# A state-space layer's sums over states, taken over transposed blocks instead of over identity products

## The reference, cut to what matters

```python
dA  = exp(dt[b,l,d] * A[d,n])
dBu = dt[b,l,d] * u[b,l,d] * Bm[b,l,n]
h   = dA * h + dBu                      # over the tokens l
y[b,l,d] = sum_n h[b,l,d,n] * Cm[b,l,n]
y   = y + u * Dp[d]
y   = y * silu(z)
out = einsum('bld,ed->ble', y, W_out)
return x + out
```

## Time and profile before

| | us |
|---|---|
| median of 3 runs | 2183.1 (2182.24 to 2184.62) |
| the profiled execution | 2189.44 |
| its span in the profile | 2187.7 |
| busy in the span: PE, DVE, ACT, POOL | 1903.7, 1653.2, 1273.8, 1450.1 |
| mean granted TensorE clock | 0.946 of full speed |
| the layer with the change in it | about 1060 to 1970 of the span |

### The profile page before, as it was taken

One profiled execution on the slowest core, in us unless ns is written; L12 is line 12 of the kernel. 1 busy time (PEld: TensorE's weight loads), 2 busy tenths in 40 slices (PEclk: granted clock), 3 DMA queues, 4 the chain that ended last, 5 costly groups with the idle time before them and its releaser, 6 DMA issues.

```text
span 2187.7 us, 32346 instructions
## 1 busy us (share of the span) xinstructions
PE 1903.7 (87%) x9878; PEld 1113.8 (51%) x9878; DVE 1653.2 (76%) x2282; ACT 1273.8 (58%) x2729; POOL 1450.1 (66%) x1195
## 2 busy tenths in 40 slices
PE   2599999999984699993799999999999999679998
PEld 1244444444433599992345454545453544248886
DVE  4477887887755555651399999999999999986664
ACT  1056666666673333333778787878787867644443
POOL 7344445443244343441499999999999999885665
PEclk9999999999885799996999999999999999889999
DMA  3545445454215354441404040404040404100100
GB/s 80 108 92 109 106 97 121 98 120 119 83 60 194 76 106 73 75 68 32 165 0 165 10 165 10 165 10 165 10 165 10 155 10 165 59 20 30 39 30 30
DMA packets 231137, 185.64 MB, mean 85 GB/s; under 512 B 148753, under 2 KB 201513, under 8 KB 230970
## 3 DMA queue, kind: packets, MB, share of 16 engines
q1 hardware_dynamic: 216090, 162.56, 25.9%
q0 software_dynamic: 13296, 17.77, 4.7%
q10 hardware_dynamic: 1584, 3.24, 0.5%
HBM read 134.02 MB, written 49.49 MB: 84 GB/s over the span
## 4 chain that ended last, share of the span: by engine, by line
POOL 28%; PE 13%; issue 7%; DVE 4%; ACT 2%; DMA 0%; POOLq 0%; DVEq 0%; ACTq 0%
POOL mb_dbu L1966 18%; PE mb_da_ps L1780 8%; POOL mb_hp L1972 8%; DVE mb_da_ps L2148 2%; PE mb_y_ps L2191 1%; DVE mb_hp L2146 1%; POOL mb_dtu L1978 1%; PE mb_f_ps L2210 1%; PE mb_f_ps L1740 1%; DVE mb_hc L2155 1%; PE mb_y_ps L1759 0%; PE mb_f_ps L2228 0%; PE mb_f_ps L2214 0%; PE mb_f_ps L2218 0%; PE mb_f_ps L1729 0%
## 5 line engine op out<-in xcount | busy, mean ns | idle before, releaser
L1966 POOL TENSOR_TENSOR mb_dbu<-mb_dtu,mb_bbc 128x1024 f32<-128x1024 f32 x256 | 600.9, 2377 | 12.9 <-DVE mb_da_ps L2148 5.8
L473 ACT ACTIVATE ex_plain<-at_t_ps 128x512 f32<-128x512 f32 x512 | 289.6, 595 | 182.8 <-PE at_t_ps L851 177.1
L2148 DVE TENSOR_TENSOR_SCAN mb_da_ps<-mb_da_ps,mb_dbu 128x1024 f32<-128x1024 f32 x160 | 365.3, 2283 | 3.5 <-ACT mb_da_ps L2018 3.3
L2191 PE MATMUL mb_y_ps<-mb_hc,lw_ident 128*128 128x512 f32 x640 | 317.3, 620 | 52.2 <-DVE mb_hc L2155 51.6
L610 DVE TENSOR_REDUCE at_mx<-at_s_ps 128x2 f32<-128x1024 f32 x256 | 311.0, 1219 | 48.5 <-PE at_s_ps L860 45.7
L860 PE MATMUL at_s_ps<-ex_w 48*128 48x512 f32 x512 | 228.8, 510 | 35.5 <-DVE at_mx L610 22.4
L851 PE MATMUL at_t_ps<-ex_w 64*128 64x512 f32 x512 | 220.7, 487 | 11.7 <-ACT ex_plain L473 6.4
L1180 POOL DMA_INDIRECT x<-m_o,m_xs x71 | 113.8, 1603 | 173.4 <-DMA x<-m_o,m_xs 105.9
L2191 PEld LDWEIGHTS mb_y_ps<-mb_hc,lw_ident 128*128 128x128 f32 x640 | 119.8, 195 | 212.9 <-issue 127.1
L1972 POOL TENSOR_TENSOR mb_hp<-mb_hp,mb_cbc 128x1024 f32<-128x1024 f32 x96 | 227.9, 2374 | 0.0
L2146 DVE TENSOR_TENSOR_SCAN mb_hp<-mb_da_ps,mb_dbu 128x1024 f32<-128x1024 f32 x96 | 218.9, 2280 | 6.5 <-POOL mb_dbu L1966 5.5
(11 more groups left out here) (339 smaller groups left out, 4160.7 us busy)
## 6 DMA issues: line engine op xcount, KB each, us to landing
mb_bbc<-mb_scr SPq DMA_DIRECT2D x64, 512.0 KB, 6.2
mb_cbc<-mb_scr SPq DMA_DIRECT2D x64, 512.0 KB, 6.4
ex_w<-at_scr SPq DMA_DIRECT2D x384, 64.0 KB, 2.2
m_xs<-rt_rows SPq DMA_DIRECT2D x71, 129.0 KB
at_scr<-at_qk_hi SPq DMA_DIRECT2D x32, 256.0 KB
at_scr<-at_qk_lo SPq DMA_DIRECT2D x32, 256.0 KB
at_xin<-in_x SPq DMA_DIRECT2D x32, 128.0 KB, 2.2
ex_plain<-in_x SPq DMA_DIRECT2D x8, 512.0 KB
```

The costliest lines, as they stand in the source:

```text
L473: act.activation(probs[:, c, h, :], t_ps[:, k % 2, :], ACT.Exp, scale=SCALE).then_inc(exp_done, 1)
L1966: pool.tensor_tensor(dbu[:, q % 3, :, :], dtu_2, bbc[:, 2 * p:2 * p + 2, :], ALU.mult).then_inc(S["dbu_ready"], 1)
L2148: dve.tensor_tensor_scan(da, da, add, 0.0, ALU.mult, ALU.add).then_inc(S["scan_done"], 1)
L2191: last = pe.matmul(y_ps[:, v % 2, :], ident[:, :], src[:, j, :], start=False, stop=(q == tile_last[v] and j == 1))
```

## The change

The unit products are transposed into the tile's bank in blocks of 128 x 128: for each of the two states, four matmuls in transpose mode with the product block as stationary operand and the identity as moving one, without starting a new accumulation, so that they add to what is there. The bank then holds, for block a, tokens on the partitions and channels on the columns. The diagonal product that starts the accumulation is turned in the same way: four fp32 matmuls with a block of u as stationary and the diagonal matrix as moving operand. When a tile is summed, ScalarE copies the bank to `u` (task `yt`), and TensorE turns it back by four transposes into the same bank (task `back`); `final` waits for that (`y_ready`) and no longer for the sums.

The tasks are put first in the list of their slot. ScalarE does `yt` of tile i at its steps 8, 16, 24 and 32 (the table's 6, 14, 22 and 30), TensorE does `back` at its steps 9, 17, 25 and, for tile 3, 1 of the next batch. The slots of `final` are not moved.

```diff
--- before.py
+++ after.py
@@ -1809,6 +1809,10 @@
     29: [("xi", 0, 2), ("bb", 6, 1), ("cb", 4, 1)], 30: [("xi", 1, 2), ("bb", 7, 1), ("cb", 5, 1), ("final", 3, 0)],
     31: [("cb", 6, 1), ("cb", 7, 1), ("dt", 1, 1), ("load", 0, 3)],
 }
+for at, i, ahead in ((6, 0, 0), (14, 1, 0), (22, 2, 0), (30, 3, 0)):
+    SCHEDULE[at].insert(0, ("yt", i, ahead))
+for at, i, ahead in ((9, 0, 0), (17, 1, 0), (25, 2, 0), (1, 3, -1)):
+    SCHEDULE[at].insert(0, ("back", i, ahead))
 MOVED = {24: [("norm_h", 0, 2)], 25: [("z", 0, 1), ("z", 1, 1)], 26: [("z", 2, 1), ("z", 3, 1)], 27: [("tr", 0, 2), ("tr", 1, 2)], 31: [("xi", 0, 2)]}
 LATER = [task for at in MOVED for task in MOVED[at]] + [("xi", 1, 2), ("silu_z", 0, 1)]
 EARLY_SCHEDULES = {-1: {at: [task for task in SCHEDULE[at] if task not in LATER] + MOVED.get(at, []) for at in SCHEDULE},
@@ -1847,7 +1851,7 @@
 
         names = """prep a_exp x_stored const_set x_loaded stats_done a_made ln_done rs_ready
                    newton norm_ready h_ready f_ready hT_hi_ready z_ready u_ready scr_written ex_steps ex_ready dt_steps dt_made dtu_ready
-                   da_ready dbu_ready scan_done hc_ready hp_ready y_summed yg_ready"""
+                   da_ready dbu_ready scan_done hc_ready hp_ready y_summed yt_ready y_ready yg_ready"""
         S = {q: sem("mb_" + q) for q in names.split()}
         layer.x_stored = S["x_stored"]
         ctx.close()
@@ -2017,6 +2021,11 @@
                         act.activation(da_ps[:, q % 2, 0, :], dt[:, d % 2, :], ACT.Exp, scale=a_neg[:, d, 2 * p:2 * p + 1])
                         act.activation(da_ps[:, q % 2, 1, 1:T], dt[:, d % 2, 1:T], ACT.Exp, scale=a_neg[:, d, 2 * p + 1:2 * p + 2]).then_inc(S["da_ready"], 1)
                     for kind, i, m in tasks(s - 2):
+                        if kind == "yt":
+                            v = ND * m + i
+                            act.wait_ge(S["y_summed"], tile_summed[v])
+                            act.wait_ge(S["dtu_ready"], v + 1)
+                            act.activation(u[:, m % 2, i, :], y_ps[:, v % 2, :], ACT.Copy).then_inc(S["yt_ready"], 1)
                         if kind == "ln":
                             act.wait_ge(S["x_loaded"], 16 * (m + 1))
                             wait(act, S["x_stored"], 16 * (m - 2))
@@ -2129,7 +2138,7 @@
                             dve.scalar_tensor_tensor(y, y, -1.0, ex[:, :], ALU.add, ALU.subtract).then_inc(S["dt_steps"], 1)
                         if kind == "final":
                             v = ND * m + i
-                            dve.wait_ge(S["y_summed"], tile_summed[v])
+                            dve.wait_ge(S["y_ready"], v + 1)
                             dve.wait_ge(S["z_ready"], m + 1)
                             dve.tensor_tensor(u[:, m % 2, i, :], y_ps[:, v % 2, :], z[:, v % 5, :], ALU.mult).then_inc(S["yg_ready"], 1)
 
@@ -2185,13 +2194,23 @@
                         if q == tile_first[v]:
                             pe.wait_ge(S["dt_made"], v + 1)
                             wait(pe, S["yg_ready"], v - 1)
-                            pe.matmul(y_ps[:, v % 2, :], diag_d[:, v % ND, :], u[:, v // ND % 2, v % ND, :], start=True, stop=False)
+                            for a in range(4):
+                                pe.matmul(y_ps[:, v % 2, a * P:(a + 1) * P], u[:, v // ND % 2, v % ND, a * P:(a + 1) * P], diag_d[:, v % ND, :], start=(a == 0),
+                                          stop=False, skip_group_check=True)
                         multiplied(pe, q)
                         for j in range(2):
-                            last = pe.matmul(y_ps[:, v % 2, :], ident[:, :], src[:, j, :], start=False, stop=(q == tile_last[v] and j == 1))
+                            for a in range(4):
+                                last = pe.matmul(y_ps[:, v % 2, a * P:(a + 1) * P], src[:, j, a * P:(a + 1) * P], ident[:, :], start=False,
+                                                 stop=(q == tile_last[v] and j == 1), is_transpose=True, skip_group_check=True)
                         last.then_inc(S["y_summed"], 1)
                     for kind, i, m in tasks(s):
                         whole = kind.removesuffix("_a")
+                        if kind == "back":
+                            v = ND * m + i
+                            pe.wait_ge(S["yt_ready"], v + 1)
+                            for a in range(4):
+                                last = pe.transpose(y_ps[:, v % 2, a * P:(a + 1) * P], u[:, m % 2, i, a * P:(a + 1) * P], ident[:, :])
+                            last.then_inc(S["y_ready"], 1)
                         if whole not in FILL_KINDS:
                             continue
                         k = fill_no[whole, i, m]
```

## The result

The changed kernel takes **2249.9 us** (median of 4 runs, 2246.5 to 2255.1) against 2183.9 for the kernel before on the same chip (4 runs, 2182.2 to 2185.0): ratio 1.0309, with an interval of 1.0296 to 1.0322. The forecast was 2264, the range 2204 to 2305.

The account below looks back on a forecast made before the run. GpSimd was taken as the bound. Delays at tile 2 of 6.2 + 1.6 + 2.5 + 2.5 = 12.8 us, less 1.2 of slack, made 11.6 per batch, 81 us over 7 batches: 2264 us, range 2204 to 2305.

Parts of the forecast that it names:

- What bounds the kernel: State-space layer: GpSimd sets the pace with 0.57 us to spare per batch; TensorE, the engine relieved, is only third.
- rival 4: Tile 2's turn is hidden: only relief is left, 4.6 us of GpSimd idle time and 2.5 in the tail, 2176; chance 0.05.
- The price of the sums: TensorE: a unit's sum falls from 1.72 to 0.88 us as eight transposes; the diagonal product in blocks takes 0.88.
- `final` of tile 2 waits for `back`: Step 26: VectorE waits for `back`, queued behind TensorE's step 24 and delayed by ScalarE's copy; 6.2 us late at full clock.
- The part at full clock: Tile 2's `final` starts at 1498.8 instead of 1492.58, 6.2 us late per batch, without any fall of the clock.
- The first fall of the clock: Thinned steps 19 to 22: TensorE drops to 1.2 GHz, costing 1.6 us before xd (z 0, unit 22) and 2.5 in xd.
- The second fall: TensorE idles from about 1487 to 1492, its clock falls again: 2.5 us in dt 0, z 1, z 2 and the sum.
- The other tiles at nothing: Turns of tiles 0, 1 and 3 cost nothing; at the lower clock tiles 0 and 3 can add 0 to 4 us per batch.
- The sum per batch: 12.8 us of delays less VectorE's 1.2 us behind GpSimd: 11.6 us per batch, 81 us over 7 batches.
- 1 (the clock holds): TensorE stays at 2.4 GHz throughout: 5.0 us per batch, 35 us in all, 2218; chance 0.18.
- 2 (a stall at tile 3 of 5.5 us): TensorE reaches steps 29 to 33 at the lower clock, tile 3's `final` waits too: 5.5 us more per batch, 2303; chance 0.10.
- rival 3: TensorE becomes the bound at 1.2 GHz all batch: 156.6 us, 47.5 more per batch, 2516; chance 0.04.

Follow-up runs that it names:

- e3: Changed kernel without ScalarE's copy and the turn back, `final` waiting for the sums themselves (output computed from transposed sums): 2182.5 us, ratio 0.9992.
- e8: Kernel before the change with one of the two halves of each unit's sum left out, ordinary products kept: 2177.7 us, ratio 0.9965.
- e1: Changed kernel with only `back` of tile 2 moved, from TensorE's step 25 to the head of its step 24: 2210.2 us, ratio 1.0113.
- e2: Changed kernel with `back` of tile 2 heading TensorE's step 24 and ScalarE's copy of tile 2 last in its step: 2201.4 us, ratio 1.0068.
- e4: Changed kernel with four more fp32 matmuls, never read, in TensorE's idle time in step 24 of the first seven batches: 2238.5 us, ratio 1.0235.
- e9: Changed kernel without copy and turn, its blocks turned by ordinary fp32 products instead of transpose mode: 2182.9 us, ratio 0.9989.

## Why the prediction was right, and where its sizes were off

- **What bounds the kernel: right.** e3 takes away 16 us of TensorE's time per batch and adds nothing, and gains 0.08% with an interval on both sides of none. The 4.6 us that I let the relief be worth in rival 4 (0.57 a batch) didn't show; the waits of the earlier trace rows stood as they were. Only e8, with a gain of 6 us that its batches don't account for, leaves something open here.
- **The price of the sums: right.** Eight transposes start 0.88 to 0.93 us ahead of what follows (1511.59 to 1512.52, 1526.17 to 1527.05). The diagonal product in blocks, for which no row stood, took 0.89 (1525.28 to 1526.17), the value taken.
- **`final` of tile 2 waits for `back`, which stands behind all of step 24 and a late xd: right in mechanism.** e1 moves nothing but that turn and gives back 7 of the 10.4 us; e2 shows the copy's share by its absence at units 26 and 28. The part at full clock was put at 6.2 us. In e4, where the clock holds from xd on, the final product still waits 4.7 and the scan of unit 26 1.6, so 6.3. Of the two banks that I had in front of `back`, the one of dt 0 held nothing up: it was free 1.5 us before z 2 (1521.93 and 1523.46), in e4 0.3 us (1523.65 and 1523.93). What held TensorE was the wait of dt 0 for the copy of xd, which also frees the bank of z 1.
- **The first fall of the clock, 1.6 for z 0 and unit 22 and 2.5 for xd: wrong.** The clock fell where forecast, in the thinned steps, but it had risen again at 1507.3, 0.7 us before xd, after TensorE had worked without a gap from 1502.49. I had assumed that xd would still be at the lower level; it took 3.63 us, as before. Of z 0 and unit 22, which did run slow, 0.4 us reached the path: xd began 0.5 us after silu of u had ended (1507.51), in e4 0.15 us after it. So of these 4.1 us 3.7 weren't there. The bound of 3.4 us for a low stretch was also read too high: the row from 1092.80 that I called continuous work is busy 5.75 of its 6.80 us.
- **The second fall, 2.5: right, and a little larger.** 6.5 us for 3.9 is 2.6, and in e4, where this fall is gone, it is 3.9 again. The batch gives back 2 of it, since another wait grows there.
- **The other tiles at nothing: too low by 1.8.** Final product of tile 3 1.0 and its L2138 0.3, scan of unit 18 0.55. They were inside the bounds of 0 to 4 that I gave for the lower clock. At tile 3 the traces bear that out: in the second batch of the changed kernel the clock is 1.00 just after the first scan (from 1188.7 on) and VectorE waits for no turn there; in the batch shown it is 0.69 (1427.5 to 1430.9), and it waits 1.0. In e2, at 0.50, it waits 2.6.
- **The sum per batch.** 12.8 + 0 - 1.2 = 11.6 forecast; 9.5 at tile 2 and 1.8 elsewhere, less the slack of 1.2, make 10.1, and 10.4 was measured. With the first and the seventh batch, which lost less (9.8 and 8.4), it is 70.3 for the 81 forecast, and the tail came out at -3.6 + 0.3 where I took 0, inside its bounds: 10.7 and 3.3 are the 14 us between forecast and median. That the -3.6 is a saving isn't shown: in e9, whose sums are as long as before, the stretch after the last scan takes 231.7 us, as with the change. And that the total came so close is partly luck: 3.7 us too much per batch at xd stood against 1.8 too little at the other tiles.
- **Rivals.** 1 (the clock holds) fell on the trace: 0.50 in two stretches a batch. Its price would have been 5.0 per batch for the place alone; e4 shows that one fall less is worth 2. 2 (a stall at tile 3 of 5.5 us) happened at a fifth of that size. 4 fell: `back` ended 17.4 us after the start of unit 24's scan (1527.65 less 1510.25), where 7.9 would have hidden it. 3 (bound at 1.2 GHz) fell by far: batch clock 0.87, TensorE 27 us idle. The Trainium skill's sentence that stood behind rival 3 ("TensorE: Matmul & The Clock Gate", Part 4: PE-mode transpose) isn't borne out by these runs: transposes ran at full clock in 1.04 us for eight (1512.52), and e3 with transposes was granted 0.89, e8 with as much work in ordinary products 0.87. In all of them ordinary products stand between the transposes; a long run of transposes alone is in none of these traces.

## What to carry to other kernels

Relief on an engine that isn't the bound was worth nothing by itself here, and a new handover between engines is priced by the queue that it is put in: a copy of 0.6 us and a turn of 0.6 for each of four tiles cost 10.4 us a batch in one set of places and, in a steady batch, 0.1 in another. So before such a change, write down for each added instruction what stands ahead of it in its engine's order and which bank or buffer that waits for; then put the result where it is ready, not where it is first needed. And where an engine is thinned out, look for its next bursts on the path: they may pay the lower clock, as dt 0 did here (6.5 us for 3.9) and xd did not.

## What of the hardware was not expected

- fp32 transposes that add up in PSUM are one MATMUL each: 0.11 to 0.12 us at the full clock back to back, about half of the 0.21 of a 128-column fp32 product (sixteen MATMULs in 1.70 us in e9 against eight in 0.96 in e3).
- TensorE's clock went down and up twice within a batch: 0.50, 1.00, 0.51, 1.00 over four stretches of 7 to 10 us, down behind 2.75 us of idle time and one unit, and within 5.20 us of it, and up again after work without a gap (from 1502.49 and from 1518.76). The busy share of a stretch itself doesn't tell its level: the first low stretch was busy 4.81 of 6.80 us, the one at 1.00 behind it 6.26 of 10.20. A kernel with TensorE 16% less busy (e3) had 0.89 in the batch and took the same time.
- Filling 3.6 us of idle time with products that nobody reads made the kernel faster by 11 us (2249.9 to 2238.5): the only gain of these runs that came from adding work.
